# Graph attention kernel: transposed scores of two heads by a second matmul, and a written order of events for each engine

## What is computed

```python
# L0: h = x @ fc_w.T + fc_b; 8 Euler steps:
h = h + dt * (sigmoid(alpha)[:, None] * 0.5 * (adj @ h - h) + h @ w_eff - h + x)
x1 = layernorm(x + h)
# L1: 4 heads of 32: q, k, v = x1 @ W
scores = q @ k.T / sqrt(32) + where(adj == 0, -inf, 0)
x2 = layernorm(x1 + softmax(scores) @ v)
```

## Time and profile before

| | us |
|---|---|
| median of 3 runs (lowest, highest) | 713.12 (711.07, 714.04) |
| the profiled execution | 711.12 |
| its span, first to last instruction | 709.3 |
| busy in the span: PE, DVE, ACT, POOL | 670.3, 442.6, 407.3, 71.0 |
| mean granted TensorE clock | 0.988 |

### The profile page before, as it was taken

The page is one execution under the profiler, slowest core; times in us unless marked ns, Lnnn a source line. Parts: engine busy times, 40 slices in busy tenths (PEclk is TensorE's granted clock), DMA queues, the critical chain, the costliest instruction groups (busy, mean ns, idle before and its releaser), DMA issues.

```text
span 709.3 us, 12335 instructions
## 1 busy us (share of the span) xinstructions
PE 670.3 (94%) x3793; PEld 506.7 (71%) x3793; DVE 442.6 (62%) x1280; ACT 407.3 (57%) x903; POOL 71.0 (10%) x85
## 2 busy tenths in 40 slices
PE   4998889999999999999999999999999999997874
PEld 3776667868777777788786877777777868675642
DVE  4442327566675757575766667575857576667774
ACT  3122237666666667566666656665766666667671
POOL 3100000001010101010010101010000101000001
PEclk9999999999999999999999999999999999999797
DMA  3000021302212130403031221303040312122120
GB/s 107 1 0 16 0 71 35 91 14 65 57 45 76 28 91 0 118 0 96 23 77 41 59 59 41 78 23 95 0 109 10 92 28 71 35 56 49 46 60 30
DMA packets 37183, 35.35 MB, mean 50 GB/s; under 512 B 7584, under 2 KB 24352, under 8 KB 37152
## 3 DMA queue, kind: packets, MB, share of 16 engines
q1 hardware_dynamic: 37152, 34.96, 19.1%
HBM read 5.57 MB, written 4.19 MB: 14 GB/s over the span
## 4 chain that ended last, share of the span: by engine, by line
PE 87%; DVE 6%; issue 3%; ACT 2%; DMA 1%; SPq 1%; POOL 0%; POOLq 0%; DVEq 0%; ACTq 0%
PE psE L700 13%; PE psL L603 9%; PE psL L605 8%; PE psL L604 8%; PE psO L711 8%; PE psS L614 8%; PE psL L595 5%; PE psL L596 5%; PE psL L597 5%; PE psM L674 4%; PE psL L665 3%; PE psM L679 2%; DVE Yl L815 2%; PE psS L542 2%; PE psL L590 2%
## 5 line engine op out<-in xcount | busy, mean ns | idle before, releaser
L449 ACT ACTIVATE E<-Sm,negmax 128x512 f32<-128x512 f32 x256 | 183.9, 719 | 115.3 <-DVE negmax L846 114.8
L846 DVE CUSTOM_DVE_ANT_0 Sm<-psS,mask 128x512 f32<-128x512 f32 x256 | 171.9, 686 | 90.8 <-PE psS L614 82.5
L700 PE MATMUL psE<-ident,E 128*128 128x128 f32 x960 | 144.1, 276 | 3.3 <-ACT E L449 3.3
L700 PEld LDWEIGHTS psE<-ident,E 128*128 128x128 f32 x960 | 117.0, 142 | 40.6 <-issue 19.6
L614 PE MATMUL psS<-Ks,Qs 96*128 96x512 f32 x256 | 116.1, 474 | 6.3 <-DVE negmax L846 3.5
L497 ACT ACTIVATE ET<-psE 128x512 f32<-128x512 f32 x120 | 70.6, 588 | 41.1 <-PE psE L700 41.1
L879 DVE COPY ET<-psE 128x512 f32<-128x512 f32 x120 | 82.3, 686 | 16.8 <-PE psE L700 16.8
L384 POOL TENSOR_TENSOR rstd<-var,minus_half 128x4 f32<-128x4 f32 x32 | 32.3, 1009 | 526.8 <-DVE var L829 526.8
L815 DVE TENSOR_TENSOR z<-psL,z 128x512 fp32r<-128x512 f32 x48 | 32.9, 691 | 52.6 <-ACT z L442 52.6
L614 PEld LDWEIGHTS psS<-Ks,Qs 96*128 96x128 f32 x256 | 47.6, 191 | 22.2 <-DVE negmax L846 15.9
L711 PE MATMUL psO<-ET,V 128*32 128x512 f32 x512 | 58.5, 595 | 1.1 <-issue 0.8
(11 more groups left out here) (137 smaller groups left out, 944.8 us busy)
## 6 DMA issues: line engine op xcount, KB each, us to landing
Qs<-qh SPq DMA_DIRECT2D x128, 64.0 KB, 2.0
Ks<-kh SPq DMA_DIRECT2D x128, 64.0 KB, 2.0
xin<-in_x_dram SPq DMA_DIRECT2D x16, 256.0 KB, 2.9
Qs<-ql SPq DMA_DIRECT2D x64, 64.0 KB, 2.0
Ks<-kl SPq DMA_DIRECT2D x64, 64.0 KB, 2.0
out_dram<-y SPq DMA_DIRECT2D x16, 256.0 KB, 2.3
E<-in_adj_dram SPq DMA_DIRECT2D x4, 256.0 KB, 4.1
W_sb<-in_L_gnn_W_dram SPq DMA_DIRECT2D x1, 192.0 KB, 4.5
```

The costliest lines, as they stand in the source:

```text
L449: nc.scalar.activation(E[:, h % 2, i, :], Sm[:, i % 2, :], ACT.Exp, scale=-1.0, bias=negmax[:, h * NT + i:h * NT + i + 1], accum_out=sums[ ...
L700: last = nc.tensor.transpose(e_bank(horner, i)[:, t * P:(t + 1) * P], E[:, n % 2, t, i * P:(i + 1) * P], ident[:, :])
L846: V_.tensor_tensor_reduce(out=Sm[:, i % 2, :], in0=psS[i % 2][:, :], in1=mask[:, i, :], scale=-SCALE, scalar=3e38, op0=ALU.add, op1=ALU.mi ...
```

## The change

1. **Transposed scores.** For heads 0 and 1 (`TH = 2`), TR(h,i) is one matmul Ks x Qs into psE: the scores of block i of the keys, already transposed. Two more rows (98 instead of 96) hold ones in Ks and in Qs the negated row maximum, high and low part, so that the maximum is subtracted in the matmul. DVE adds a transposed mask `maskT` from PSUM to ET, ACT takes exp in place in ET. The exp of S(h,i) remains for the row sums, and is written back to Sm.
2. **The maximum rows.** MT: when heads 0 and 1 have their maxima, PE transposes negmax (128x8), ACT and DVE split it in Mh and Ml, SP copies them by two DMAs to rows 96 and 97 of Qs. TR(0,0) waits for them. The DVE add of TR(0,0) also waits for PV of the batch before.
3. **maskT** is made at the start: 16 transposes of adj behind iteration 0, and four DVE instructions.
4. **Heads 2 and 3** keep the transposes. ACT now makes all eight copies, and shares them with DVE only for the last two batches.
5. **u** is gone: UT goes to psM and LN1A and LN1B read PSUM.
6. **Order.** Each engine has a list of its own. The last number of an event is the lag of its batch. S of head 0, head 1 and half of head 2 now come one iteration earlier (lag 1), PV(0) too (lag 2).
7. **Behind the last iteration** each engine has one list (`*_DRAIN`) whose last number is the batch.

```diff
-EVENTS = [
-    ("HORNER", 0, 0), ("UT", 0, 0), ("S", 1, 0), ("PV", 0, 0), ("PV", 1, 0), ("PV", 2, 0), ("PV", 3, 0),
...
+PE_EVENTS = [
+    ("PV", 1, 0, 3), ("PV", 2, 0, 3), ("PV", 3, 0, 3), ("S", 2, 2, 2), ("UT", 0, 0, 1), ("S", 2, 3, 2),
...
+SP_EVENTS = [
+    ("STK", 0, 0, 2), ("STK", 1, 0, 2), ("OUT", 0, 0, 4), ("STK", 2, 0, 2), ("STK", 3, 0, 2), ("XIN", 0, 0, 0),
+    ("MT", 0, 0, 2),
...
+def schedule(table, drain, g, j):
+    if isinstance(g, int) and g == NG:
+        for kind, n, i, b in drain:
+            yield kind, n, i, b, b % IPG
+    else:
+        for kind, n, i, lag in table:
+            b = g * IPG + j - lag
+            if not isinstance(g, int) or b >= 0:
+                yield kind, n, i, b, (j - lag) % IPG
...
+                    elif kind == "MT":
+                        sp.wait_ge(mt_lo, b + 1)
+                        for row, part in enumerate((Mh, Ml)):
+                            sp.dma_start(f(Qs[KS + row:KS + row + 1, 0:TH, :]), f(part[:, :])).then_inc(mt_in, 16)
...
-                nc.scalar.activation(E[:, h % 2, i, :], Sm[:, i % 2, :], ACT.Exp, scale=-1.0,
+                row = Sm[:, i % 2, :]
+                nc.scalar.activation(row if h < TH else E[:, h % 2, i, :], row, ACT.Exp, scale=-1.0,
...
+                    elif kind == "TR" and n < TH:
+                        act.wait_ge(t_ev[i % 2], (b * H + n) * (NT // 2) + i // 2 + 1)
+                        nc.scalar.activation(ET[:, n, i, :], ET[:, n, i, :], ACT.Exp, scale=SCALE).then_inc(st_exp, 1)
...
+                        if n < TH:
+                            last = mm(e_bank(b, n, i)[:, :], Ks[0:KT, n, i * P:(i + 1) * P], Qs[0:KT, n, :],
+                                      start=True, stop=True)
+                        else:
+                            for t in range(NT):
...
+                    elif kind == "MT":
+                        pe.wait_ge(m_ev, MPB * (b + 1))
+                        pe.wait_ge(s_max, s_unit(b, TH, 0))
+                        nc.tensor.transpose(psM[0:TH * NT, 0:P], negmax[:, 0:TH * NT], ident[:, :]).then_inc(mt_mm, 1)
...
-                        moments(0, p, lambda t: u[:, t, :])
+                        moments(0, b, lambda t: psM[:, t * P:(t + 1) * P])
...
+                    elif kind == "TR" and n < TH:
+                        if n == 0 and i == 0 and after_first(b):
+                            dve.wait_ge(o_mm, b)
+                        dve.wait_ge(t_mm, s_unit(b, n, i) + 1)
+                        V_.tensor_tensor(ET[:, n, i, :], e_bank(b, n, i)[:, :], maskT[:, i, :],
+                                         ALU.add).then_inc(t_ev[i % 2], 1)
```

More of the change, by code:

```diff
@@ new lines @@
+ACT_EVENTS = [
[8 rows of a table added]
+]
+DVE_EVENTS = [
[8 rows of a table added]
+]
+POOL_EVENTS = [
+    ("XS", 0, 0, 0), ("LN1A", 0, 0, 0), ("KEEP", 0, 0, 0), ("LN2A", 0, 0, 2),
+]
+SP_EVENTS = [
+    ("STK", 0, 0, 2), ("STK", 1, 0, 2), ("OUT", 0, 0, 4), ("STK", 2, 0, 2), ("STK", 3, 0, 2), ("XIN", 0, 0, 0),
+    ("MT", 0, 0, 2),
+]
+PE_DRAIN = [
[13 rows of a table added]
+]
+ACT_DRAIN = [
[11 rows of a table added]
+]
+DVE_DRAIN = [
[13 rows of a table added]
+]
+POOL_DRAIN = [
+    ("LN2A", 0, 0, 14), ("LN2A", 0, 0, 15),
+]
+SP_DRAIN = [
+    ("STK", 0, 0, 14), ("STK", 1, 0, 14), ("OUT", 0, 0, 12), ("STK", 2, 0, 14), ("STK", 3, 0, 14),
+    ("MT", 0, 0, 14), ("STK", 0, 0, 15), ("STK", 1, 0, 15), ("STK", 2, 0, 15), ("STK", 3, 0, 15),
+    ("MT", 0, 0, 15), ("OUT", 0, 0, 13), ("OUT", 0, 0, 14), ("OUT", 0, 0, 15),
+]
@@ L101, in run_iterations, with after_first @@
+PE_DRAIN_HEAD = (14, 0, 0)
+MPB = 4
+def schedule(table, drain, g, j):
[7 more added lines that the diff above has]
+                yield kind, n, i, b, (j - lag) % IPG
+def after_first(b):
+    return not isinstance(b, int) or b > 0
 def run_iterations(eng, iteration):
-    iteration(0, 0, True, False, False, False)
@@ L104, in run_iterations @@
[L104 to L106 removed]
+    for g in range(2):
+        for j in range(IPG):
+            iteration(g, j)
     with eng.Fori(2, NG - 1) as g:
         for j in range(IPG):
[L109 removed]
+            iteration(g, j)
     for j in range(IPG):
[L111 to L113 removed]
@@ L114, in run_iterations @@
-    iteration(NG + 1, 0, False, False, False, True)
+        iteration(NG - 1, j)
+    iteration(NG, 0)
 def carry_waits(eng, passed):
@@ L272, in f, with late, e_bank @@
             return ap.bitcast(F32)
[L274 to L279, removed]
+        def late(b, h, i):
+            return isinstance(b, int) and (b, h, i) >= PE_DRAIN_HEAD
+        def e_bank(b, h, i):
+            return (psE + psL)[i] if late(b, h, i) else psE[i % 2]
         def l0_unit(it, piece):
@@ L311, in _ @@
             sp.dma_start(xin[:, 0:1, :, :], x_v[:, 0:1]).then_inc(xin_in[0], 16)
[L313 to L318, removed]
-                    sp.dma_start(xin[:, 1 - j:2 - j, :, :], x_v[:, bass.ds(it + 1, 1)]).then_inc(xin_in[1 - j], 16)
-                def store():
-                    sp.wait_ge(y_done, it - END + 1)
-                    sp.dma_start(out_v[:, bass.ds(it - END, 1)],
-                                 y[:, :, :].rearrange("p (o t) d -> p o t d", o=1)).then_inc(y_out, 16)
-                def stack(dst, parts, h):
-                    rows = slice(h * HD, (h + 1) * HD)
-                    for r, part in enumerate(parts):
-                        sp.dma_start(f(dst[r * HD:(r + 1) * HD, h, :]),
-                                     f(part[rows, :])).then_inc(stacked[h], 16)
-                if end and (horner or not prep):
-                    store()
-                if prep:
-                    for h in range(H):
-                        if attend:
-                            sp.wait_ge(s_mm, s_unit(it - ATT, h, NT))
-                        if h == 0:
-                            sp.wait_ge(m_ev, MPB * (it - PREP) + 2)
-                        stack(Qs, (qh, ql, qh), h)
-                        if h == 0:
-                            sp.wait_ge(m_ev, MPB * (it - PREP) + 3)
-                        stack(Ks, (kh, kh, kl), h)
-                        if not horner and h == 1:
-                            store()
@@ L611, in scores @@
                     pe.wait_ge(stacked[h], 6 * 16 * (a + 1))
-                if not fresh or i >= 2:
+                if isinstance(s, int) and s == 0:
+                    pe.wait_ge(c_vec, 5 + NT)
+                    pe.wait_ge(ones_in, 1)
+                if not isinstance(s, int) or s >= 2:
                     pe.wait_ge(s_max, s - 1)
@@ L721, in iteration @@
                         last.then_inc(c_mm, 1)
+                if isinstance(g, int) and g == 0 and j == 0:
+                    for m in range(NT):
+                        for t in range(NT):
+                            last = nc.tensor.transpose(P_BANKS[m][:, t * P:(t + 1) * P],
+                                                       adj_sb[:, t, m * P:(m + 1) * P], ident[:, :])
+                        last.then_inc(a_mm, 1)
             run_iterations(pe, iteration)
```

312 lines of the change are left out of this document (171 added, 141 removed), and 77 rows, old and new, of tables (ACT_DRAIN, ACT_EVENTS, DVE_DRAIN, DVE_EVENTS).

## The result

The changed kernel takes 684.4 us (median of 4 runs, 683.4 to 685.6) against 712.1 us of the kernel before on the same chip: ratio 0.961, 95% interval 0.958 to 0.965. The forecast was 684.

A forecast was written before the change was run, and what follows sets the result against it. It took PE to bound the loop and chains to set the time behind it: 711.12 - 18.9 (loop) + 1.6 (start) - 12.0 (end) = 681.8, with 2.0 to the median 684 us; range 677 to 692.

The forecast's parts named there:

- Loop: -18.9 forecast: Part 1: iterations 4 to 15 gain 17.0 us at 37.1 each, iterations 2 and 3 together 1.9.
- 8 x 0.205 = 1.64 us off PE: Loop, per iteration: eight TR go from 0.44 us as transposes to 0.235 as a matmul.
- I take 0.1 of net waiting: Loop: waits add 0.1 us to 37.0, giving 37.1 per iteration, bounds 36.7 and 38.1.
- The tight places: Loop: X1T, K, J1 and TR(3,2) have spare 0.1 us or 0; all others 0.3 or more.
- spare 0.1: Loop, X1T at 7.8 us of the iteration: LN1B is done at about 7.6, leaving 0.1 us.
- waits for QL: Loop, K at 13.3 us of the iteration: QL, queued on DVE, is done at about 13.3, spare 0.
- 0.2 more: Loop: LN1B reading PSUM instead of SBUF may take 0.2 us more; bounds 0 and 0.2 per iteration.
- Start: +1.6 forecast: Part 2: adj transposes and six more S lengthen the start, partly taken up by PE's idle time; bounds 0 and 3.2 us.
- End: -12.0 forecast: Part 3, behind the last iteration: 56 us for 68.0, with the last batch starting 10 us earlier; bounds 53 and 62.
- The 2 us of TR(0,0) for the maximum rows: End: TR(0,0) of batch 15 waits 2 us for head 3's stack and MT's rows, which land at 29.6.
- Rival: the rows land late: Loop: TR(0,0) waits for the maximum rows; with waits of 2.5 us 719 us in all, chance 0.06.
- Rival: the loop gains nothing: Loop: QL, X1T and J1 each late by 0.3 to 0.5 us, pushing the next; 692 to 703 us, chance 0.17.

The follow-up runs named there:

- e1: Changed kernel with four fp32 transposes of a constant in place of each matmul that writes a transposed score tile of heads 0 and 1: 698.4 us.
- e6: Changed kernel with CB moved behind two score matmuls, UT ahead of S(2,2), QL ahead of the maxima of S(3,1), K ahead of S(3,3): 678.5 us.
- e7: Changed kernel with the old path of the update: ScalarE copies it from PSUM to u in SBUF and VectorE reads that: 691.6 us.
- e12: Changed kernel with only UT moved ahead of the score matmul S(2,2) on TensorE: 681.0 us.
- e9: Kernel before, with only the steps that prepare batch 15 in the last part moved as early as they can stand: 713.7 us.
- e10: e6 with the low part of Z1 earlier on VectorE, Q one transposed tile earlier and S(3,3) one later on TensorE: 681.8 us.
- e8: Changed kernel with UT of batch 15 behind the four PV groups of batch 13, its sums behind the maxima of S(2,3): 689.0 us.

## Why the prediction was right, and where not

The number held, and each of its three parts is near. But the loop's came out right by two errors that cancel.

- **Loop: -18.9 forecast, -18.3 found; 37.1 per iteration forecast, 37.1 found.** The step "8 x 0.205 = 1.64 us off PE" is right as a price (0.47 for a free pair; transposes 0.40 to 0.44 each in e1), but only 1.14 of it reaches the time in this order (e1). "I take 0.1 of net waiting" was mis-sized: the new waits are 0.5. On the other side, MT costs 0.20 for the 0.15 taken, and no term stood for the waits that the new order removes, 0.5: 0.31 of it is J1's, which the forecast saw and kept. That makes the 0.30 of e1 against before. 0.4 too little here and 0.45 too much there make a hit, and that is luck.
- **The tight places.** X1T "spare 0.1" is 0.30 late. K "waits for QL" is right: the weight load has this wait 14 times in the trace, 4.5 us in all, 0.3 each, of which 0.13 reaches PE. J1 doesn't wait: its first matmul takes 0.31, as fp32r matmuls behind four transposes do elsewhere in the loop (0.31 to 0.32). Not on the list was the second pair of transposed scores, 0.08. e6, e7 and e12 show that one chain is behind X1T and K.
- **LN1B from PSUM, "0.2 more".** 1.36 for 1.11 us, 0.25. The estimate from the Trainium skill (VectorE: DVE Perf Modes, "Why PSUM operands drop a tier") was 0.27 for 512 elements; the trace agrees. What neither said: the path over `u` costs more, +0.39 per iteration (e7). Reading PSUM is a gain.
- **Start: +1.6 forecast.** Iteration 2 starts at about 109.2, so the start took 3.2 more, the forecast's upper bound. What it had wrong is the wait of X1T in iteration 1, taken as now: it is 2.35 us (before 0.71), since the new order leaves PE less to do ahead of X1T. And this wait has a second price that the forecast didn't have. In the repeat of the changed kernel the clock falls behind it; the windows are of the first trace and of the repeat:

```profile
85.00:90.00 5.00, 4.75 (x23) 3.46 (x21) 1.45 (x3) 1.70 (x4) 0.35 (x1) 1.00 0.03 9
```

```profile
85.00:90.00 5.00, 4.33 (x14) 2.91 (x15) 1.28 (x4) 1.39 (x3) 0.61 (x1) 0.66 0.00 0
```

  From X1T to the first mark the repeat takes 59.6 us for 58.4. So 1.2 of the 2.2 us between the two starts are the clock. In ten of the twelve traces with the new order (all but before and e9) this window has 0.66 to 0.75, in the changed kernel's first and in e10 1.00.
- **End: -12.0 forecast, -12.5 found.** First S of batch 15 forecast at +16.4, found at +15.1. The 2 us of TR(0,0) for the maximum rows never came: the rows were issued at 653.40 and 654.12, their 1.9 us end at 656.0, and TR(0,0) was due at 657.2. In their place the tail is longer, 14.3 us for 13.3, where the forecast took it as unchanged: LN2B of batch 14 now stands ahead of batch 15's division on DVE, which starts 5.8 us behind the start of PV for 5.0. That the end's gain is one of order and not of the matmul was the forecast's reasoning; e1 (93.4 for 93.7) and e8 (+5) support it, within what the clock blurs.
- **Rival: the rows land late.** Forecast spare 2.9 us, found 3.8. The rule of the Trainium skill on how many DMA engines such a transfer gets (DMA: Bandwidth & Descriptors) has no visible price here: 1.9 us from issue to use, no longer than the stacks' 2.0. The forecast's count of two engines by that rule isn't borne out either: the trace has eight packets of 512 bytes for each of the two transfers, and its semaphore rises once early and then in eight steps. The order of SP lists the transfer as 1x8x128, which fits eight and not two. The price that the rival set for a wait was too low: 2.81 us of it cost 4.3, not 2.8.
- **Rival: the loop gains nothing.** Its mechanism, one chain on DVE's order, is what took 0.4 of the 0.5 us in each iteration. It was far smaller than the 1.2 that it was given.
- **The bound of 0.91 for a tile.** It is one fourth of PV, and PV is 16 matmuls for all four quarters, not for each quarter as the description of the kernel has it; the trace lists them as 32 records.

Open: what the old tail would gain at an undisturbed clock (e9), what holds the second pair of transposed scores, and whether e6's rest at X1T can be had; that wasn't tried.
